# One block for the routed feed-forward and the agent attention of a two-layer decoder, streamed in groups of four batches

## The reference, cut to what matters

```
def _L0_ffn_ref(x, Wg, We, be):              # third: routed feed-forward
    h = x.reshape(n, d);  cap = n // E       # n = 3584 rows, E = 8, cap = 448
    probs = softmax(h @ Wg, axis=1); best = argmax(probs)
    mask = one_hot(best, E); gate = sum(probs * mask)
    locations = cumsum(mask, axis=0) - 1.0   # place of a row in its expert
    mask = mask * (locations < cap)
    ...                                      # every expert has the same We, be
    return gate * (h @ We + be)              # 0 for rows beyond cap (in effect)

def _L1_attn_ref(x, w_qkv, w_conv1):         # fourth: agent attention, batch by batch
    q, k, v = split(x @ w_qkv.T)
    agent = einsum('bnc,c->bn', q, w_conv1)
    agent_attn = softmax(einsum('bn,bnc->bc', agent * scale, k))
    agent_v = softmax(einsum('bc,bnc->bn', agent_attn, v))
    agent_v = einsum('bn,bnc->bc', agent_v, v)
    return softmax(agent[:, :, None], axis=-1) * agent_v[:, None, :]
```

## Time and profile before

| | |
|---|---|
| Median of 3 runs | 3393.48 us (3384.04 to 3399.62) |
| Profiled execution | 3393.12 us |
| Its span, first to last instruction | 3391.3 us |
| Busy: TensorE, VectorE, ScalarE, GpSimd | 85%, 60%, 46%, 12% of the span |
| Mean granted TensorE clock | 0.891 of 2.4 GHz |
| `sf_` and `ag_` blocks with the layernorm between | 1625.4 to 2005.9 us, 380.5 us |

### The profile page before, as it was taken

How to read it: one execution, slowest core, us unless ns; L and a number is a source line. 1 busy time by engine, 2 the same in 40 slices (tenths; PEclk the granted TensorE clock), 3 DMA queues, 4 the chain that set the end, 5 groups by cost and what they waited for, 6 DMA issues and landing times. The chain is left out here.

```text
span 3391.3 us, 62686 instructions
## 1 busy us (share of the span) xinstructions
PE 2893.5 (85%) x21120; PEld 1909.7 (56%) x21121; DVE 2024.0 (60%) x4546; ACT 1544.2 (46%) x3150; POOL 408.4 (12%) x405
## 2 busy tenths in 40 slices
PE   4788888886699999998886867999999867869994
PEld 1344444443367766776556754777777634436663
DVE  2388888887277777776224344777777634563334
ACT  1465665552266666664112313666666332211222
POOL 0000000000200000000000012011011022214441
PEclk8889999998799999998555578999999889988997
DMA  3000000000000000000000001000000030001115
GB/s 89 0 0 0 0 0 0 0 0 1 26 24 18 18 23 18 18 18 1 4 0 13 0 6 46 19 23 23 18 23 18 1 128 13 12 21 46 64 62 155
DMA packets 57533, 80.49 MB, mean 24 GB/s; under 512 B 8593, under 2 KB 46660, under 8 KB 57092
## 3 DMA queue, kind: packets, MB, share of 16 engines
q1 hardware_dynamic: 51380, 62.55, 6.3%
q0 software_dynamic: 6048, 16.52, 1.5%
HBM read 63.46 MB, written 15.60 MB: 23 GB/s over the span
## 5 line engine op out<-in xcount | busy, mean ns | idle before, releaser
L1016 DVE CUSTOM_DVE_ANT_0 xa_h_scores<-xa_h_score_bank,xa_h_added 112x375 f32<-112x375 f32 x1024 | 518.1, 544 | 152.7 <-PE xa_h_score_bank L951 138.2
L1110 ACT ACTIVATE xa_h_probs<-xa_h_scores,xa_h_negmax 112x375 f32<-112x375 f32 x1024 | 561.4, 600 | 0.8 <-DVE xa_h_negmax L1023 0.6
L963 PEld LDWEIGHTS xa_h_turn_bank<-keep_ident,xa_h_probs 112*125 112x125 f32 x3072 | 398.4, 190 | 91.3 <-ACT xa_h_probs L1110 22.3
L963 PE MATMUL xa_h_turn_bank<-keep_ident,xa_h_probs 112*125 112x112 f32 x3072 | 438.3, 279 | 8.7 <-DVE xa_h_probs_t L1030 8.5
L1030 DVE COPY xa_h_probs_t<-xa_h_turn_bank 125x448 f32<-125x448 f32 x512 | 319.1, 623 | 150.9 <-PE xa_h_turn_bank L963 137.8
L1116 ACT ACTIVATE xa_h_probs_t<-xa_h_turn_bank 125x448 f32<-125x448 f32 x256 | 138.8, 542 | 303.7 <-PE xa_h_turn_bank L963 303.7
L358 PE MATMUL mb_y_bank<-mb_read_out,keep_ident 128*128 128x448 f32 x512 | 231.2, 600 | 25.6 <-DVE mb_read_out L560 25.5
L553 DVE TENSOR_TENSOR_SCAN mb_state<-mb_decay,mb_drive 128x1792 f32<-128x1792 f32 x64 | 248.5, 3883 | 2.1 <-ACT mb_decay L487 2.1
L951 PE MATMUL xa_h_score_bank<-xa_h_keys,xa_h_queries 32*112 32x375 f32 x2048 | 230.9, 520 | 11.4 <-DVE xa_h_row_max L1016 10.7
L976 PEld LDWEIGHTS xa_h_sums_bank<-xa_h_probs_t,xa_h_values 125*32 125x32 f32 x6144 | 141.9, 110 | 154.4 <-DVE xa_h_probs_t L1030 149.2
L976 PE MATMUL xa_h_sums_bank<-xa_h_probs_t,xa_h_values 125*32 125x112 f32 x6144 | 202.6, 265 | 14.6 <-issue 6.3
(11 more groups left out here) (330 smaller groups left out, 4544.4 us busy)
## 6 DMA issues: line engine op xcount, KB each, us to landing
xa_h_context<-in_ctx_t SPq DMA_DIRECT2D x64, 375.0 KB, 3.1
lm_w<-in_m_w SPq DMA_DIRECT2D x16, 512.0 KB
lm_e_wide<-lm_result_rows SPq DMA_DIRECT2D x8, 896.0 KB, 9.5
keep_x<-in_x SPq DMA_DIRECT2D x4, 896.0 KB, 11.2
lm_latent_rows<-lm_rows SPq DMA_DIRECT2D x8, 448.0 KB, 3.2
out_x<-keep_x SPq DMA_DIRECT2D x8, 448.0 KB, 6.1
xa_h_mask_raw<-in_key_mask SPq DMA_DIRECT2D x1, 1312.5 KB
mb_f_pw<-in_pw SPq DMA_DIRECT2D x1, 1024.0 KB
```

The costliest lines, as they stand in the source:

```text
L963: last = pe.transpose(turn_bank[(par + kc) % 2][0:KP, g * S:(g + 1) * S], probs[par][:, g, kc * KP:(kc + 1) * KP], keep.ident[0:S, 0:S])
L1016: dve.tensor_tensor_reduce(scores[par][:, g, :], score_bank[g][0:S, 0:SK], added[s][:, :], 1.0, -BIG, ALU.add, ALU.max, row_max[par][:, g: ...
L1110: act.activation(probs[par][:, g, :], scores[par][:, g, :], ACT.Exp, bias=negmax[s][:, G * c + g:G * c + g + 1]).then_inc(probs_ready, 1)
```

## The change

The two blocks become one, `switch_and_agent` (names `sa_`); the layernorm block between them (`n4_`) is gone. Groups of four batches stream through both sublayers in an unrolled loop:

- routing is done for each group (`route`, `weigh`), and the count of earlier rows for each expert is carried from group to group in `earlier`;
- ScalarE normalises (`normalise_rows`) in place of VectorE, and VectorE adds the expert's result to x straight out of PSUM (`update`);
- the second layernorm is made for each group (`scales`), with a power of -0.5 on GpSimd and one refining step on VectorE;
- the normalised tokens and their transposes are kept for all batches (`tokens`, `tokens_t`), so that they are made once where they were made three times and twice;
- scores and gather become two stretches of 64 source matmuls of one column, and the value is made once for all batches (L1414) and spread over rows with matmuls of 32 contraction rows in four bands (L1422), which VectorE adds four batches at a time (L1629).

The group's bias matmul is 512 columns for two batches. The block loads 14 tensors by DMA at its start, where the two blocks loaded 4 and 5; the first eight of them are waited for before the first transpose.

```diff
-PHASES = (1, 2, 3, 4, 5, 6,)
+PHASES = (1, 2, 3, 5, 6,)
...
-def switch_ffn(nc, keep, name, w):
+def switch_and_agent(nc, keep, name, w):
...
+        banks = psum("banks", [128, 8, 512])
+        out_psum = [[banks[0:S, 2 * n + b // 2, b % 2 * D:(b % 2 + 1) * D] for b in range(G)] for n in range(2)]
+        turn_psum = [banks[:, 4 + c, 0:T] for c in range(DC)]
...
+            def turn_rows(g):
...
+            def expert(g, half):
+                reuse(pe, updated, G * (g - 2) + 2 * half + 2)
+                bank = banks[0:S, 2 * (g % 2) + half, :]
+                pe.matmul(bank, ones[32 * half:32 * half + 1, :], expert_b[32 * half:32 * half + 1, :], start=True, stop=False)
+                for b in (2 * half, 2 * half + 1):
                     for c in range(DC):
...
+                        last = pe.matmul(out_psum[g % 2][b], normed_t[g % 2][:, c, b * S:(b + 1) * S], expert_w[:, c, :],
+                                         start=False, stop=b % 2 == 1 and c == DC - 1)
+                last.then_inc(expert_done, 1)
...
+            def number_places(g):
+                pe.wait_ge(chosen_ready, g + 1)
+                pe.matmul(places_psum, upto[:, :], chosen[g % 2][:, :, 1:], start=True, stop=False)
+                pe.matmul(places_psum, ones[:, :], earlier[g % 2][:, :, 0:G], start=False, stop=True).then_inc(places_done, 1)
...
+            turn_rows(0)
+            for t in range(GROUPS + 2):
+                if in_range(t):
+                    gate_logits(t)
+                if in_range(t + 1):
+                    turn_rows(t + 1)
+                if in_range(t):
+                    expert(t, 0)
+                    number_places(t)
+                if in_range(t - 2):
+                    sum_tokens(t - 2)
+                if in_range(t - 1):
+                    turn_tokens(t - 1)
+                if in_range(t):
+                    expert(t, 1)
...
+                if in_range(t - 1):
+                    agent_scores(t - 1)
...
+            for b in range(B):
+                for c in range(DC):
+                    last = pe.matmul(banks[0:S, 3, b:b + 1], tokens_t[:, c, b // G, b % G * S:(b % G + 1) * S], channel_w[:, c, b:b + 1],
                                      start=c == 0, stop=c == DC - 1)
             last.then_inc(pe_step, 1)
...
+            for b in range(B):
+                for c in range(DC):
+                    last = pe.matmul(banks[:, 2, c * B + b:c * B + b + 1], tokens[:, b, c * 128:(c + 1) * 128], token_weights[:, b:b + 1],
+                                     start=True, stop=True)
+            last.then_inc(pe_step, 1)
...
+            pe.wait_ge(act_step, 8)
+            pe.wait_ge(own_step, 6)
+            for g in range(GROUPS):
+                reuse(pe, x_added, g - 1)
+                for r in range(4):
+                    band = slice(32 * r, 32 * (r + 1))
+                    last = pe.matmul(banks[0:S, 4 * (g % 2) + r, 0:D], own_wide[band, g, :], agent_v[band, :], start=True, stop=True)
+                last.then_inc(value_done, 1)
...
+            normalise_rows(0)
+            read_rows(0)
+            normalise_rows(1)
+            for t in range(GROUPS + 2):
+                if in_range(t - 1):
+                    normalise_tokens(t - 1)
+                if in_range(t + 1):
+                    read_rows(t + 1)
+                if in_range(t):
+                    exponentials(t)
+                if in_range(t - 2):
+                    act.wait_ge(sum_done, t - 1)
+                    act.activation(token_sum[:, :, G * (t - 2):G * (t - 1)], token_sum_psum, ACT.Copy).then_inc(sum_ready, 1)
+                if in_range(t - 1):
+                    read_tokens(t - 1)
+                if in_range(t + 2):
+                    normalise_rows(t + 2)
...
+                pool.wait_ge(scaling, SCALING * g + 2)
+                pool.tensor_tensor(rstd2[:, here], variance2[:, here], power[:, :], ALU.pow).then_inc(rooted, 1)
...
+                dve.tensor_tensor(pick[:, :, 1:].rearrange("p e b -> p b e"), kept[:, :, :], wide(best), ALU.is_equal).then_inc(routing, 1)
+                if g > 0:
+                    dve.tensor_copy(pick[:, :, 0], earlier[1 - g % 2][:, :, G]).then_inc(routing, 1)
                 else:
...
+                    dve.memset(pick[:, :, 0], 0.0).then_inc(routing, 1)
+                dve.wait_ge(routing, at + 6)
+                dve.tensor_tensor_scan(before[:, :, :].rearrange("p e b -> p (e b)"), reset[:, :], pick[:, :, :].rearrange("p e b -> p (e b)"), 0.0,
+                                       ALU.mult, ALU.add).then_inc(chosen_ready, 1)
...
+            for t in range(GROUPS):
+                route(t)
+                weigh(t)
+                update(t, 0)
+                update(t, 1)
+                scales(t)
...
+            for g in range(GROUPS):
+                here = keep.x[:, G * g:G * (g + 1), :]
+                dve.wait_ge(value_done, g + 1)
+                dve.tensor_tensor(here, banks[0:S, 4 * (g % 2):4 * (g % 2) + 4, 0:D], here, ALU.add).then_inc(x_added, 1)
+                dve.wait_ge(x_added, g + 1)
+                for t in range(G * g, G * (g + 1)):
+                    dve.bn_stats(keep.stats[:, t, :], keep.x[:, t, :])
...
-            switch_ffn(nc, keep, "sf_", t)
-        if 4 in PHASES:
-            layernorm_scales(nc, keep, "n4_")
-            agent_attention(nc, keep, "ag_", t)
```

More of the change, by code:

```diff
@@ new lines, in sum_tokens @@
+            def sum_tokens(g):
+                pe.wait_ge(agent_ready, g + 1)
+                for b in range(G):
+                    for c in range(DC):
+                        last = pe.matmul(token_sum_psum[:, c, b:b + 1], tokens[:, G * g + b, c * 128:(c + 1) * 128], agents[:, G * g + b:G * g + b + 1],
+                                         start=True, stop=True)
+                last.then_inc(sum_done, 1)
+            pe.wait_ge(loaded, 16 * 8)
+            pe.wait_ge(constants, 2)
+            turn_rows(0)
@@ L1506, in _ @@
             for c in range(DC):
[L1507 removed]
+                last = pe.transpose(banks[:, 1, c * B:(c + 1) * B], key_probs[:, c * 128:(c + 1) * 128], keep.ident[0:B, 0:B])
             last.then_inc(pe_step, 1)
@@ new lines, in _ @@
+            pe.wait_ge(dve_step, 4)
+            pe.transpose(banks[0:S, 1, 0:B], token_probs[:, :], keep.ident[0:B, 0:B]).then_inc(pe_step, 1)
+            pe.wait_ge(act_step, 6)
+            for b in range(B):
+                for c in range(DC):
+                    last = pe.matmul(banks[:, 2, c * B + b:c * B + b + 1], tokens[:, b, c * 128:(c + 1) * 128], token_weights[:, b:b + 1],
+                                     start=True, stop=True)
+            last.then_inc(pe_step, 1)
+            pe.wait_ge(act_step, 7)
@@ new lines, in _ @@
+            for c in range(DC):
+                last = pe.matmul(banks[:, 3, 0:D], gathered[:, c, :, :].rearrange("p r b -> p (r b)"), wv_t[:, c, :], start=c == 0, stop=c == DC - 1)
+            last.then_inc(pe_step, 1)
+            pe.wait_ge(act_step, 8)
[6 more added lines that the diff above has]
+                last.then_inc(value_done, 1)
@@ new lines, in normalise_tokens, with read_rows @@
+            def normalise_tokens(g):
+                act.wait_ge(scales_ready, g + 1)
+                for b in range(G):
+                    t = G * g + b
+                    act.activation(tokens[:, t, :], keep.x[:, t, :], ACT.Identity, bias=shift2[:, t:t + 1],
+                                   scale=rstd2[:, t:t + 1]).then_inc(tokens_ready, 1)
+            def read_rows(g):
+                reuse(act, expert_done, 2 * (g - 1))
+                for c in range(DC):
+                    act.wait_ge(turned, DC * g + c + 1)
+                    act.activation(normed_t[g % 2][:, c, :], turn_psum[c], ACT.Copy).then_inc(turned_read, 1)
@@ L1621, in update @@
+            def update(g, half):
+                dve.wait_ge(expert_done, 2 * g + half + 1)
+                for b in (2 * half, 2 * half + 1):
+                    t = G * g + b
+                    dve.scalar_tensor_tensor(keep.x[:, t, :], out_psum[g % 2][b], weight[:, t:t + 1], keep.x[:, t, :],
                                              ALU.mult, ALU.add).then_inc(updated, 1)
-                for s in range(G):
-                    t = G * i + s
+                for b in (2 * half, 2 * half + 1):
+                    t = G * g + b
@@ L1657, in _ @@
-            with dve.Fori(1, B // G) as i:
-                rows_of(2, i)
-                update(i)
+                dve.wait_ge(small_step, 2 * (at > 0) + 2)
+                dve.tensor_scalar(probs, exps_of, stat[:, at + 3:at + 4], None, ALU.mult).then_inc(dve_step, 1)
+            dve.memset(ones[:, :], 1.0).then_inc(constants, 1)
+            for e in range(E):
+                last = dve.memset(preference[:, e:e + 1], float(E - e))
+            last.then_inc(constants, 1)
```

(5 more changed lines are left out.)

543 lines of the change are left out of this document (201 added, 342 removed).

## The result

| | before | after |
|---|---|---|
| Median | 3389.93 us (3384.04 to 3399.62, 4 runs) | 3270.02 us (3261.6 to 3271.82, 4 runs) |
| Ratio | 1 | 0.9639 (95% interval 0.9609 to 0.9669) |
| Span of the profiled execution | 3391.3 us | 3269.6 us |
| Busy: TensorE, VectorE, ScalarE, GpSimd | 85%, 60%, 46%, 12% | 86%, 61%, 47%, 13% |
| Mean granted clock | 0.891 | 0.902 |

The kernel is 3.6% faster, 3270 us where 3276 was forecast and 3240 to 3322 was the range. The profile of the kernel after, busy time by stage. The columns are the stretch, its length, the busy time of TensorE, its weight loads, VectorE, ScalarE and GpSimd with their instructions, then TensorE's granted clock, the DMA share and GB/s.

The account below looks back on a forecast made before the run. TensorE was taken to set the pace, mostly at clock 0.50. Start 7.8, loop 150.4 and tail 104.9 us sum to 263.1 for 380.5 us, a gain of 117.4, so 3276 us; range for 8 in 10, 3240 to 3322 us.

Parts of the forecast that it names:

- Start: Block start to the loop: DMA issues and landing, first group's transposes and last copy, 7.8 us.
- loop: All eight groups up to the last expert run: 147.4 us at clock 0.62, with the first turn 150.4 us.
- tail: Behind the last expert run, at clock 0.50: remaining scores and sums, softmaxes, token scores, gather, value and spreading, 104.9 us.
- Work at full clock in the loop: TensorE's instructions over all eight groups of the loop, priced at 182.8 us at clock 0.50; durations halve at 1.0.
- The clock, 0.62: TensorE's granted clock in the new loop, half way between 0.50 and the third pass's 0.75; bounds 0.50 and 0.85.
- rival one: The clock never rises in the loop: loop 185.8 us, time 3311 us; chance 0.21.
- Rivals one and two: The second: clock up most of the loop, at 0.85, time 3236 us, chance 0.14; rival one has its own line.
- the 0.57: Loop clock if transposes ahead of a run do not help it rise: 160 us, 10 us more; not taken.
- rival three: Loop bound by the chain between engines, VectorE's turn behind TensorE's work: at most 62 us more, 3330 us; chance 0.10.
- rival four: GpSimd's power is dear in VectorE's 7.7 us turn, binding from about 11 us; 3427 us at 30 us; chance 0.03.
- GpSimd's power: Inverse root for each group in the loop, taken as 0.5 us, bounds 0.1 and 1.2 us.
- Pipeline rest: First part of the tail: last two groups' scores and sums, one set of transposes, copies; 16.2 us.

Follow-up runs that it names:

- runs_split: Against the kernel after, each batch's bias (halved to 256 columns) and two expert matmuls stand alone between light matmuls; 3300.9 us, ratio 0.9743.
- bias_rows: Against the kernel after, the bias matmuls use 112 contraction rows, all but one zero, in place of one row; 3225.9 us, ratio 0.9505.
- turns_more: Against the kernel after, 64 unused transposes of the tokens are added in one piece ahead of the token scores; 3284.7 us, ratio 0.9692.
- power_30: Against the kernel after, GpSimd computes each group's inverse root 30 times over; 3476.2 us, ratio 1.0253.
- loops_apart: Against the kernel after, the one loop is cut in two again with the same instructions; 3270.8 us, ratio 0.9650.
- value_each: Against the kernel after, each batch again has its own two 256-column value matmuls and VectorE adds each batch separately; 3285.0 us, ratio 0.9687.

## Why the prediction was right

- **The sum.** 264.9 us measured for 263.1. Start 6.8 for 7.8, loop 156.3 for 150.4, tail 101.9 for 104.9, so that errors of 6 us one way and 4 the other stand against each other. The time came out 6 us under the forecast although the stretch was 1.8 us over it: the rest is the 6.1 us outside the block.
- **Work at full clock in the loop.** 182.8 us at 0.50 is 91.4; measured 92.2. The durations of before carried over: a run of two 3.59 for 3.6, bias 2.04 for 1.98. That they halve at 1.00, as the sum took it, is nearly so: 1.98 and 1.11 us.
- **The clock, 0.62 against 0.59.** The forecast took it half way between two rows for want of a rule. That the size came out near is luck. The picture behind it (a rise after about every second run) does not hold: rises stand at both ends of the loop, with 78.5 us at 0.50 between. That the one-row bias beside each run would be what decides was named only as support for rival one. The runs show how wide the term was: by order, nearly alone, 0.50 to 0.67, by the bias's rows 0.79, by wider matmuls 0.98. Rivals one and two (3311 and 3236 us) are within reach of small edits; runs_split and bias_rows took 3301 and 3226.
- **The Trainium skill's rule on transposes.** That the full clock does not engage for transposes (TensorE: Matmul & The Clock Gate, Part 4: PE-mode transpose) was weighed at 10 us (the 0.57 that the forecast took for it gives 160.4 us for 147.4, so 13) and set aside on the rows; turns_more bears that out.
- **VectorE beside TensorE, rival three.** Its 47.9 us are covered. In power_30 its turn, with its waits for ScalarE and TensorE, is 15.8 us and not 7.7; rival four's sum left these waits out. The cover at 0.59 was some 4 us a turn (4.9 less the 1.0 of the power), much less than the sum made it; it was enough.
- **GpSimd's power.** 1.01 us where 0.5 was taken, within 0.1 to 1.2, and hidden.
- **The tail.** Pipeline rest 15.9 for 16.2 (at a clock of 0.61 where 0.50 was taken, but with TensorE idle for 3.6 us where 1.5 was), key softmax 6.7 for 7.1, token scores 24.4 for 24.1, gather 28.0 for 28, second softmax 2.5 for 4.3, value 2.6 for 2.7, spreading 21.9 for 22.5. The softmax's row of before held VectorE work that is not there now (2.17 us busy, 0.82 after).
- **Where the gain comes from.** About 31 of the 120 us are the loop's clock: with it at 0.50 throughout, runs_split takes 3301 us. The sum had this in the 0.62, the list of where the gain comes from did not name it. The waits and VectorE's pass that went are seen by stage in loops_apart, and the value edit in value_each (8.9 us by stage, 15 by the medians). What the routing's count by group alone or the dropped second layernorm alone is worth was not run; it is read from stages only.

## What to carry to other kernels

When TensorE is busy from end to end, price a loop as its full-clock work divided by the granted clock, and treat the clock as a term of its own with wide bounds: here the order of the same work, with the biases cut or side by side, moved it from 0.50 to 0.67 and the time by 50 us. A loop at 0.50 with TensorE 99% busy is a place to look: giving the matmuls of one and of eight columns 112 columns cost 3 us of full-clock work in the loop and gave 85 us in all, giving the one-row ones 112 rows gave 44. The two do not add up. Merging two loops for cover is worth only what was uncovered, and the profile of each loop shows that beforehand: TensorE was busy for 93% and 99% of the two.

## What the runs showed of the hardware

- A matmul with one contraction row does not help the clock as one with 112 rows does, all but one of them zero: the same 512 columns, mean clock in the loop 0.59 and 0.79, 44 us.
- Two one-row matmuls of 512 columns in different row bands (0 and 32) take as long as one: 1.04 us up to the next matmul at 1.00. Two with 112 rows take 1.72. A single one with 112 rows takes 0.86.
- 64 transposes and nothing else took the clock from 0.50 to 1.00 within 7.76 us.
- One-column matmuls stay at 0.50 at 99% busy (24.05 of 24.35 us); with 112 columns the same 128 records took 15.2 us for 24.4.
- A power of 112x4 elements on GpSimd takes 1.01 us; 30 in a row took 29.4.
